# TensorE's chunk loop written out, and the gram units taken two at a time

## What is computed

```
dots = einsum('bfd,bgd->bfg', x, x)              # x: 2048 x 27 x 128, a 27x27 gram per sample
h = concat([x_mlp, dots[lower triangle], 0])     # 128 + 351 + 1 = 480 columns
for w, b in (480->1024, 1024->1024, 1024->512, 512->256):
    h = relu(h @ w.T + b)
y = h @ w_out.T + b_out                          # 2048 x 1
```

## Time and profile before

| | |
|---|---|
| median of 3 runs | 543.13 us (541.19 to 544.7) |
| the profiled execution | 541.43 us, of which the span from first to last instruction is 539.3 us |
| mean granted TensorE clock | 0.971 |
| PE busy | 508.7 us (94% of the span) |
| PEld / DVE / ACT / POOL busy | 479.5 / 171.5 / 166.6 / 132.8 us |
| DMA | 54.00 MB, mean 100 GB/s |

### The profile page before, as it was taken

The page is one execution under the profiler, slowest core; times in us unless marked ns, Lnnn a source line. Parts: engine busy times, 40 slices in busy tenths (PEclk is TensorE's granted clock), DMA queues, the critical chain, the costliest instruction groups (busy, mean ns, idle before and its releaser), DMA issues.

```text
span 539.3 us, 18870 instructions
## 1 busy us (share of the span) xinstructions
PE 508.7 (94%) x7595; PEld 479.5 (89%) x7595; DVE 171.5 (32%) x384; ACT 166.6 (31%) x380; POOL 132.8 (25%) x242
## 2 busy tenths in 40 slices
PE   6786899999999799989999899997999999999998
PEld 5575898999999799978999799997999999999997
DVE  1155635444313432142312333133322443123110
ACT  3245534334212332133222242223321342123112
POOL 1610311213222231212222132221312132223221
PEclk9687999999999999998999899998999999999999
DMA  8987967757665356553574446653565543300000
GB/s 233 240 267 161 251 98 114 137 97 117 101 119 95 59 91 106 121 89 50 91 121 93 69 77 95 115 98 60 85 105 121 91 75 62 68 28 2 1 0 1
DMA packets 281098, 54.00 MB, mean 100 GB/s; under 512 B 265126, under 2 KB 279230, under 8 KB 281022
## 3 DMA queue, kind: packets, MB, share of 16 engines
q1 hardware_dynamic: 279090, 52.22, 51.0%
q10 hardware_dynamic: 1932, 0.61, 0.5%
HBM read 45.71 MB, written 7.09 MB: 98 GB/s over the span
## 4 chain that ended last, share of the span: by engine, by line
PE 84%; DMA 7%; SPq 4%; issue 2%; DVE 1%; ACT 1%; ACTq 0%
PE acc L668 73%; PE gram_ps L626 8%; DMA rows<-in_r_bottom_output_dram 4%; SPq L439 2%; DMA pairs<-blocks 2%; DMA blocks<-grams 1%; SPq L421 1%; PE gram_ps L594 1%; DVE xt L844 1%; PE side_ps L599 1%; ACT h_full L763 1%; PE acc L599 1%; PE side_ps L689 0%; PE side_ps L594 0%; PE side_ps L642 0%
## 5 line engine op out<-in xcount | busy, mean ns | idle before, releaser
L668 PE MATMUL acc<-h_a,w_hi 128*128 128x256 f32 x1152 | 225.5, 289 | 0.0
L668 PEld LDWEIGHTS acc<-h_a,w_hi 128*128 128x128 f32 x1152 | 183.9, 191 | 2.8
L668 PE MATMUL acc<-h_a,w_lo 128*128 128x256 f32 x576 | 158.6, 283 | 0.0
L763 ACT ACTIVATE h_full<-acc,small_t 128x256 f32<-128x256 f32 x175 | 83.4, 477 | 240.7 <-PE acc L668 240.2
L539 POOL TENSOR_TENSOR h_a<-h_full,h_a 128x256 fp32r<-128x256 f32 x96 | 72.3, 753 | 213.0 <-DVE h_a L856 213.0
L668 PE MATMUL acc<-x,w_hi 128*128 128x256 f32 x504 | 107.9, 301 | 15.6 <-issue 11.6
L668 PEld LDWEIGHTS acc<-h_a,w_lo 128*128 128x128 f32 x576 | 110.3, 192 | 0.0
L668 PEld LDWEIGHTS acc<-x,w_hi 128*128 128x128 f32 x504 | 86.0, 201 | 18.2 <-issue 12.4
L668 PE MATMUL acc<-h_b,w_hi 128*128 128x256 f32 x512 | 101.2, 289 | 0.0
L539 POOL TENSOR_TENSOR h_b<-h_full,h_b 128x256 fp32r<-128x256 f32 x64 | 47.3, 739 | 172.4 <-DVE h_b L856 172.4
L668 PEld LDWEIGHTS acc<-h_b,w_hi 128*128 128x128 f32 x512 | 82.2, 191 | 0.9
(11 more groups left out here) (54 smaller groups left out, 179.0 us busy)
## 6 DMA issues: line engine op xcount, KB each, us to landing
rows<-in_r_bottom_output_dram SPq DMA_DIRECT2D x444, 64.0 KB, 2.1
blocks<-grams SPq DMA_DIRECT2D x30, 216.0 KB, 4.0
w_raw<-in_L_rec_w_dram SPq DMA_DIRECT2D x6, 1024.0 KB, 8.0
early_rows<-in_r_bottom_output_dram SPq DMA_DIRECT2D x12, 224.0 KB, 5.8
stage_pairs<-in_L_rec_w_dram SPq DMA_DIRECT2D x1, 1408.0 KB, 11.5
w_raw<-in_L_rec_w_dram SPq DMA_DIRECT2D x2, 512.0 KB, 8.0
mlp_rows<-r_bottom_mlp_output_dram SPq DMA_DIRECT2D x8, 128.0 KB, 3.2
pairs<-blocks SPq DMA_DIRECT2D x8, 126.0 KB
```

The lines of the kernel that those rows point to most:

```text
L668: last = nc.tensor.matmul(acc_slot(c, slot), weight(wp, layer, m, k), in_tile(layer, k, xp), start=(k == 0 and n == 0), stop=(k == K_TILES ...
L763: nc.scalar.activation(h_full[:, slot % 2, :], acc_slot(c, slot), ACT.Relu, bias=small_t[:, slot:slot + 1]).then_inc(drained, 1)
```

## The change

TensorE's program has no loop any more: all eight chunks are written out one after the other. The other engines keep their loops. The hooks now hold two units each and stand 36 products apart where one unit stood every 18 products. The units that are transposed ahead are 4 (2 hooks) where they were 5. In chunk 0 the hooks with units stand 5 places (30 products) apart where they stood 2 places (12 products) apart for one unit each; the last grams of chunk 1 are made at place 46 where they were made at place 38. SP's order of loads follows: 4 units and not 5 are loaded behind the gather.

```diff
-HOOK, FIRST_HOOK = 18, 6
+HOOK, FIRST_HOOK, UNITS_A_HOOK = 36, 6, 2
 W1_EARLY, FIRST_UNIT, LATE_HOOK = 7, 6, 22
-AHEAD, AHEAD_HOOK = 5, 46
+AHEAD, AHEAD_HOOK = 2, 48
+AHEAD_UNITS = AHEAD * UNITS_A_HOOK
 FULL_ROWS = 112
 EARLY_SLOTS, SHORT_LAG = 8, 2
-OUT_HOOK, EARLY_TILES = 2, 4
+OUT_HOOK, EARLY_TILES = 1, 4
...
-    if n < UNITS:
-        steps.append(("raw", ahead, n))
-    if n >= UNIT_LAG:
-        steps.append(("gram", ahead, n - UNIT_LAG))
+    for i in range(UNITS_A_HOOK):
+        if n < UNITS // UNITS_A_HOOK:
+            steps.append(("raw", ahead, n * UNITS_A_HOOK + i))
+    for i in range(UNITS_A_HOOK):
+        if n >= UNIT_LAG:
+            steps.append(("gram", ahead, (n - UNIT_LAG) * UNITS_A_HOOK + i))
     return steps
...
-UNIT_HOOKS = UNITS + UNIT_LAG
+UNIT_HOOKS = UNITS // UNITS_A_HOOK + UNIT_LAG
...
-    places = [FIRST_UNIT + 2 * i for i in range(UNIT_HOOKS)]
+    places = [FIRST_UNIT + 5 * i for i in range(UNIT_HOOKS)]
...
-        hooks[AHEAD_HOOK + 3 * n] += unit_steps(n, 2)
+        hooks[AHEAD_HOOK + 6 * n] += unit_steps(n, 2)
...
-                for u in range(ROWS_RING if start else ROWS_RING + AHEAD, UNITS):
+                for u in range(ROWS_RING if start else ROWS_RING + AHEAD_UNITS, UNITS):
...
-                    for u in range(ROWS_RING, ROWS_RING + AHEAD):
+                    for u in range(ROWS_RING, ROWS_RING + AHEAD_UNITS):
...
-            chunk(0)
-            with pe.Fori(1, CHUNKS - 2) as c:
+            for c in range(CHUNKS):
                 chunk(c)
-            chunk(CHUNKS - 2)
-            chunk(CHUNKS - 1)
             out_row(CHUNKS - 1)
```

## The result

The changed kernel takes 510.03 us in the median of 4 runs (506.94 to 511.38), beside 543.1 us before; the ratio is 0.9384, with a 95% interval of 0.9332 to 0.9437. The profiled execution took 510.51 us, with a span of 508.4. So 33 us went, where 38 were forecast; the range of 500 to 517 holds the time.

The account below looks back on a forecast made before the run. The kernel was taken to be bound by TensorE's stream. Savings of 16.9 + 18.5 + 1.1 = 36.5 us off the 539.3 us span gave 502.8, with 2.1 around it 504.9, called 505 us; range 500 to 517.

Parts of the forecast that it names:

- What bounds it: Whole kernel: bound by TensorE's stream, PE busy 508.7 of 539.3 us; only what shortens or stops that stream counts.
- Term 1: TensorE's loop, chunks 1 to 5: four taken branches, with the slower clock behind them, cost 16.9 us; written out, all goes.
- Term 2: Units in chunks: two side by side save 0.33 us a pair, so 56 pairs save 18.5 us (10.6 to 20.2).
- the bounds: What a pair's second unit adds: at least 0.215 us, at most 0.385; 0.246 was taken.
- Term 3: Chunk 0: PE's 1.5 us wait for DVE before chunk 1's first grams goes, less 0.4 us: net 1.1 us.
- What was held to be hidden: Paired copies, loads, later spill and gather, other engines' branches: all covered by slack, so nothing was taken for them.
- The anchor: The sum starts from the profiled span of 539.3 us plus 2.1 around it; that execution is 1.7 below the runs' median.
- The rule on matmuls of few columns: Small matmuls in units: some 60 cycles each, 0.8 us for a unit's 32, pairing loses some 12 us; no chance given.
- The dear second unit: Rival on pairs: the second unit costs 0.385 us like the first, saving 10.6 for 18.5, so 513 us; chance 0.17.
- Late pairs: Rival: spill and gather take 6.5 us longer, TensorE stops 1 to 2 us in seven chunks: 512 to 519; chance 0.12.
- Gaps that stay: Rival at chunk boundaries: the gaps come from the last drains, not the branch, and remain: 522 us; chance 0.05.
- slow fetch: Rival: fetching TensorE's fresh straight code cannot keep up and stops five chunks: 563 us, slower than before; chance 0.03.

Follow-up runs that it names:

- waits ahead of the pair: The changed kernel, but TensorE's waits for both units of a pair stand ahead of the pair's first matmul, none between its units: 508.43 us.
- the second profile: Profile of the changed kernel run again without any edit: span 504.3 us, against 508.4 in its first profile.
- the repetition: The changed kernel run again without any edit, beside the last kernels on the same chip: 507.96 us, ratio 0.936.
- four units: The changed kernel, but with grams of four units at a time every 72 products, transpositions still in pairs every 36: 504.10 us.

## Why the prediction was right, and what in it was off

- **What bounds it.** Right from chunk 1 on: only TensorE's stream counted, and the gains are seen in its chain. In chunk 0 it also waits for DVE and for rows, by 0.5 to 6.7 us in the two profiles of the changed kernel (66 to 90 us), and in the second one the chain there runs through SP and the DMAs.
- **Term 1, the branch, 16.9 us.** Right in the distances and in the medians (542.5 to 525.6 alone), gap and clock together. The method carried it: the distance between two equal events with and without a branch, not the length of the "issue" pieces, which is 9.2 us for all four of before and leaves out the clock.
- **Term 2, two units together, 18.5 us.** The mechanism was right, the size was off. A pair saves (58.64 - 56.47) / 8 = 0.271 us, not 0.33: 56 pairs give 15.2 us, 3.3 less. The step that failed is the value chosen between the bounds: the pitch of one unit's loads (7.7 ns) doesn't hold for the next unit's (9.4), so the second unit costs 0.30 and not 0.246. The argument that half clock showed one pitch for three units said nothing of full clock. The waits between the units, which were to leave no trace, leave none (waits ahead of the pair).
- **Term 3, chunk 0, 1.1 us.** The mechanism was right: the wait of 1.5 us is gone with pairs and back with single units. The size held in the mean of the profiles as far as their scatter lets one see; the single profile of the changed kernel had new waits of 6.7 us there that the prediction did not name, and the second profile had 0.5.
- **What was held to be hidden.** Right from chunk 1 on: pairs in time, no wait for an accumulator, SP in time. The spill in chunk 2 was issued 36.8 us after the chunk's first product (reckoned from the output row), where 37 was worked out. Not right for chunk 0: its spill was to get no later because SP had 3.5 us to spare for the grams. But the spill follows SP's row loads, before and after. It was issued 1.6 us later in the first profile (104.38 against 102.74) and only 2.1 us earlier in the second (100.63), where TensorE's output row came 6.8 us earlier; there TensorE waits 0.47 us for the pairs.
- **The anchor.** The sum was made on the profiled execution (541.43), which was 1.7 us under the median, and I took the gap for something that would go with the clock falls. It did not: from the median, 543.1 - 16.9 - 15.2 - 1.1 = 509.9, and 510.0 was measured. That it meets to 0.1 us is luck, since the interval is some 3 us wide on either side and the repetition gave 508.0. The 5 us between forecast and result are 3.3 of term 2 and 1.7 of this.
- **The rule on matmuls of few columns** was rightly given no chance: four units, 128 loads and matmuls, take 1.28 us, some 10 ns each. The Trainium skill's rule of some 60 cycles for each matmul (TensorEngine Tiling (Array Packing), Instruction Overhead) does not hold here.
- **Rivals.** The dear second unit (0.385) was half right: 0.30 lies between. Late pairs came at the start of chunk 1 alone, for 0 to 1.2 us in the six profiles with pairs and not in seven chunks. Gaps that stay and slow fetch did not come.

What stays open: why further units' loads come at 9.4 ns and not 7.7, whether the clock's fall behind a gap can be foreseen, why a branch costs more with pairs and stops TensorE a second time there, and what sets the 4 us of scatter in chunk 0.

## What to carry to other kernels

Where a bound engine runs a long loop body, measure a taken branch by the distance between equal events with and without it, and write the loop out if the program may grow: here 4.2 us for each branch in the mean with single units, 5.5 and 6.6 with pairs. Runs of small matmuls between large ones are best gathered, because each run costs 0.19 us for the change and back, and a further unit in a row costs 0.30 us instead of 0.385; the four PSUM banks held a run of four units here, and a longer one was not tried. When the bound engine gets faster, follow the data that it needs next back to the engine that issues its transfer: here, in chunk 0, SP's row loads came earlier by 2.1 us where TensorE did by 6.8. Take the pitch of a long run from a long run at the same clock, and anchor the sum to the median.

## What the hardware showed that was not expected

A pause of some 3 us on TensorE can cost up to twice its length: in the kernel with pairs and loop a gap of 3.4 us was followed by 6 us at 1.2 GHz, and four branches cost 22 us, in the kernel before 17. The clock fell behind a gap of 2.62 us and not behind one of 2.92. TensorE's branch, with a body of a chunk, takes 3.6 to 3.8 us in the median and 4.2 at most, and 2 to 3 packets of 16 KB are loaded anew for each; ACT's takes 45 ns.
